# A recurrence over eight chunks: the query output of a chunk placed behind the next chunk's rounds, and the small weight renormalised second

## What is computed

```
def step(carry, xs):
    W0, W1, W2 = carry
    qi, ki, vi, li = xs
    l0, l1, l2 = (li[..., 0], li[..., 1], li[..., 2])
    gq = silu(jnp.einsum('bhd,bcd->bhc', W0, qi))
    hq = jnp.einsum('bhd,bcd->bhc', W2, qi)
    o = jnp.einsum('boh,bhc->bco', W1, gq * hq)
    gba = jnp.einsum('bhd,bcd->bhc', W0, ki)
    hbm = jnp.einsum('bhd,bcd->bhc', W2, ki)
...
    dw0, dw1, dw2 = (newton_schulz5(dw0), newton_schulz5(dw1), newton_schulz5(dw2))
    W0 = renorm(W0 + dw0, n0)
    W1 = renorm(W1 + dw1, n1)
    W2 = renorm(W2 + dw2, n2)
    return ((W0, W1, W2), o)
```

## Time and profile before

| what | value |
|---|---|
| median of 3 runs | 1986.2 us (1982.34 to 1986.29) |
| the profiled execution, its own time | 1982.01 us |
| its span, first to last instruction | 1980.3 us |
| mean granted clock of PE over the span | 0.914 of full speed |
| busy: PE, DVE, ACT, POOL | 88%, 70%, 40%, 55% of the span |

### The profile page before, as it was taken

The page is one execution under the profiler, slowest core; times in us unless marked ns, Lnnn a source line. Parts: engine busy times, 40 slices in busy tenths (PEclk is TensorE's granted clock), DMA queues, the critical chain, the costliest instruction groups (busy, mean ns, idle before and its releaser), DMA issues.

```text
span 1980.3 us, 35242 instructions
## 1 busy us (share of the span) xinstructions
PE 1745.4 (88%) x13630; PEld 948.8 (48%) x13630; DVE 1392.0 (70%) x2440; ACT 792.9 (40%) x1181; POOL 1095.0 (55%) x644
## 2 busy tenths in 40 slices
PE   4888751948999999999999999999999999995893
PEld 3666641834444444444444444444444444443482
DVE  3666654347787777887777877778778887786474
ACT  3444420533444444444444444444444444441131
POOL 2232204032777677776767767777677777682303
PEclk8886755969999999999999999999999999996897
DMA  7000000210000000000000000000000000003122
GB/s 243 4 3 3 3 1 30 62 38 1 1 1 1 1 1 1 1 1 1 1 1 1 1 1 1 1 1 1 1 1 1 1 1 1 1 1 99 32 58 60
DMA packets 41533, 32.76 MB, mean 17 GB/s; under 512 B 3604, under 2 KB 37392, under 8 KB 41368
## 3 DMA queue, kind: packets, MB, share of 16 engines
q1 hardware_dynamic: 31096, 22.12, 3.6%
q0 software_dynamic: 2048, 4.20, 0.7%
q10 hardware_dynamic: 8224, 4.19, 0.7%
HBM read 18.96 MB, written 11.53 MB: 15 GB/s over the span
## 4 chain that ended last, share of the span: by engine, by line
PE 81%; DVE 9%; issue 5%; POOL 3%; ACT 1%; DMA 1%; SPq 0%; DVEq 0%; POOLq 0%; ACTq 0%
PE psum L1781 23%; PE psum L1766 20%; PE psum L1740 8%; PE psum L1760 6%; PE psum L1407 2%; PE psum L1796 2%; PE psum L1790 2%; PE psum L1181 1%; PE psum L1713 1%; PE psum L1193 1%; PE psum L1367 1%; DVE a_mx L1945 1%; POOL a_acc L2077 1%; PE psum L1417 1%; PE psum L447 1%
## 5 line engine op out<-in xcount | busy, mean ns | idle before, releaser
L2077 POOL TENSOR_TENSOR a_acc<-a_acc,a_Pb 128x832 f32<-128x832 f32 x448 | 893.3, 1994 | 307.8 <-ACT a_Pb L1883 275.1
L1945 DVE TENSOR_REDUCE a_mx<-psum 128x2 f32<-128x1024 f32 x512 | 625.5, 1224 | 237.2 <-PE psum L1740 234.2
L1883 ACT ACTIVATE a_Pb<-psum 128x1024 f32<-128x1024 f32 x512 | 496.7, 1022 | 703.5 <-PE psum L1766 701.5
L1781 PE MATMUL psum<-a_Pb,a_Vb 128*64 128x512 f32 x2048 | 494.3, 604 | 0.0
L1996 DVE TENSOR_TENSOR a_acc<-a_acc,a_Pb 128x192 f32<-128x192 f32 x448 | 230.9, 515 | 28.9 <-ACT a_Pb L1883 5.4
L1781 PEld LDWEIGHTS psum<-a_Pb,a_Vb 128*64 128x64 f32 x2048 | 127.2, 136 | 244.7 <-issue 173.7
L1740 PE MATMUL psum<-a_Kh,a_Qh 64*128 64x512 f32 x1024 | 231.3, 447 | 8.4 <-DVE a_mx L1945 8.3
L1766 PE MATMUL psum<-a_Qh,a_Kh 64*128 64x512 f32 x1024 | 231.1, 447 | 0.0
L1766 PE MATMUL psum<-a_Ql,a_Kh 64*128 64x512 f32 x1024 | 203.8, 393 | 0.0
L1740 PEld LDWEIGHTS psum<-a_Kh,a_Qh 64*128 64x128 f32 x1024 | 97.1, 184 | 222.6 <-issue 211.6
L1766 PE MATMUL psum<-a_Qh,a_Kl 64*128 64x512 f32 x1024 | 203.4, 392 | 0.0
(11 more groups left out here) (385 smaller groups left out, 2004.0 us busy)
## 6 DMA issues: line engine op xcount, KB each, us to landing
x_rows<-zero ACTq DMA_DIRECT2D x2, 2048.0 KB, 20.9
g_w<-in_L_ffn_w_eDF_dram SPq DMA_DIRECT2D x2, 1408.0 KB, 8.7
r_W<-in_L_ffn_W_dram SPq DMA_DIRECT2D x1, 2048.0 KB, 12.4
r_tile_x<-x_rows SPq DMA_DIRECT2D x16, 128.0 KB, 2.1
y_rows<-r_tile_y SPq DMA_DIRECT2D x16, 128.0 KB, 1.8
g_tile_x<-x_rows SPq DMA_DIRECT2D x16, 128.0 KB, 2.2
y_rows<-g_tile_y SPq DMA_DIRECT2D x16, 128.0 KB, 1.8
g_w<-in_L_ffn_w_eFD_dram SPq DMA_DIRECT2D x2, 512.0 KB, 10.5
```

The lines of the kernel that those rows point to most:

```text
L1781: last = pe.matmul(ps[HEAD[h], B_O, :], b.Vb[:, p // 2 % 2, kc, at], b.Pb[:, step % BUFS, h * QT:(h + 1) * QT], start=(kc == 0), stop=(kc ...
L1883: act.activation(b.Pb[:, step % BUFS, :], ps[:, slot:slot + 2, :].rearrange("p a b -> p (a b)"), ACT.Exp, scale=SCALE).then_inc(S["probs"], 1)
L1945: v.tensor_reduce(b.mx[:, :, qc, quarter:quarter + 1], ps[:, bank:bank + 2, :], AX.X, ALU.max).then_inc(S[f"free{bank}"], 1)
L2077: g.tensor_tensor(b.acc[:, u, at], before, b.Pb[:, step % BUFS, at], ALU.add).then_inc(S["added_pool"], 1)
```

## The change

1. PE issues `forward_output(c - 1)` at the end of iteration c, behind the two matmuls of the row sums, and no longer between the query products and the gradients. W1's transposed copy `W1T` gets two buffers for this.
2. The output no longer goes from PSUM to DVE. ACT copies it to a new tile `o` (`keep_output`, L520 of the new text), after the table load that ends iteration c. POOL adds the residual in iteration c + 1, behind the scaling of queries and keys, and DVE takes the statistics (`stats(c - 2)`) in that same iteration. The products of the next chunk wait for the copy.
3. The gate of the previous chunk moves behind `db` and `hb` on ACT, and behind `dh` and `hd` on POOL. `db` and `dh` now come before `hb` and `hd`.
4. The last additions, the renormalisations and the products go in the order W0, W1, W2 (`PRODUCT_ORDER`). The rounds go in the order 0, 1, 2.
5. POOL's three products with the rates (`rate`) and the blocks are issued after the third polynomial of rounds 0, 1, 2 and 3, and no longer in a row.

The diff, cut to what the prediction speaks of:

```diff
@@ ttt_pe, products @@
             pe.wait_ge(S["w1_kept"], c)
+            if c > 1:
+                pe.wait_ge(S["output_kept"], c - 1)
...
-        for m in range(3):
+        for n, m in enumerate(PRODUCT_ORDER):
             if c:
-                pe.wait_ge(S["moved"], 3 * (c - 1) + m + 1)
+                pe.wait_ge(S["moved"], 3 * (c - 1) + n + 1)
+                if n == 1:
+                    pe.wait_ge(S["norms"], 3 * c + 2)
@@ ttt_pe, main loop @@
         query_products(c)
-        if c:
-            forward_output(c - 1)
-        pe.wait_ge(S["scaled"], c + 1)
+        pe.wait_ge(S["scaled"], 3 * c + 3)
...
         row_sums(c, 0)
         row_sums(c, 1)
+        if c:
+            forward_output(c - 1)
@@ ttt_act @@
+    def keep_output(c):
+        act.wait_ge(S["output"], c + 1)
+        if c > 1:
+            act.wait_ge(S["residual"], c - 1)
+        act.activation(t.o[:, c % 2, :], ps[:, B_OUT, 256:512], ACT.Copy).then_inc(S["output_kept"], 1)
...
     for c in range(NC - 1):
-        if c:
-            gate(c - 1)
         act.wait_ge(S["products"], 3 * c + 1)
         act.activation(t.sig[:, :, :], products_at(ps, 0), ACT.Sigmoid).then_inc(S["products_out"], 1)
         act.wait_ge(S["products"], 3 * c + 3)
+        act.activation(t.db[:, :, :], products_at(ps, 2), ACT.Copy).then_inc(S["products_out"], 1)
         act.activation(t.hb[:, :, :], products_at(ps, 1), ACT.Copy).then_inc(S["products_out"], 1)
-        act.activation(t.db[:, :, :], products_at(ps, 2), ACT.Copy).then_inc(S["products_out"], 1)
+        if c:
+            gate(c - 1)
...
         act.activation(t.warm[:, 2 + c % 2:3 + c % 2], k.eps[:, 0:1], ACT.Sigmoid)
+        if c:
+            keep_output(c - 1)
     gate(NC - 2)
+    keep_output(NC - 2)
@@ ttt_dve @@
         head_squares(c + 1)
-        if c:
-            residual(c - 1)
         scales(c + 1)
+        if c > 1:
+            stats(c - 2)
         for n, m in enumerate(NS_ORDER):
             v.wait_ge(S["grad_squares"], 3 * c + n + 1)
...
-    residual(NC - 1)
+    for c in range(NC - 3, NC):
+        stats(c)
@@ ttt_pool @@
+    def residual(c):
+        g.wait_ge(S["output_kept"], c + 1)
+        at = slice(TPC * c, TPC * c + TPC)
+        g.tensor_tensor(k.y_all[:, at, :], t.o[:, c % 2, :].rearrange("p (a b) -> p a b", a=TPC), k.x_all[:, at, :], ALU.add).then_inc(S["residual"], 1)
...
         if c:
             gate(c - 1)
...
         scale(c + 1)
-        if c < NC - 2:
-            rates(c + 1)
-        if c:
-            blocks(c)
+        if c > 1:
+            residual(c - 2)
+        for it in range(NI - 1):
+            g.wait_ge(S["G"], 15 * c + 3 * it + 3)
+            if it < 3 and c < NC - 2:
+                rate(c + 1, it)
+            if it == 3 and c:
+                blocks(c)
```

More of the change, by code:

```diff
@@ L441, in ttt_pe @@
                 pe.wait_ge(S["X"], 7 * c + 3 + it)
-                if c and it == 0:
-                    pe.wait_ge(S["residual"], c)
                 for n, m in enumerate(NS_ORDER):
@@ L455, in ttt_pe @@
                 pe.wait_ge(S["X"], 7 * c + 7)
-                for m in range(3):
-                    pe.wait_ge(S["G"], at + (1 if m == 0 else 3))
+                for n, m in enumerate(PRODUCT_ORDER):
+                    pe.wait_ge(S["G"], at + (1 if n == 0 else 3))
                     for h in range(HEADS):
@@ L613, in scales, with stats @@
         v.tensor_tensor(s2v, s2v, rb, ALU.mult).then_inc(S["scales"], 1)
-    def residual(c):
-        v.wait_ge(S["output"], c + 1)
-        v.tensor_tensor(k.y_all[:, TPC * c:TPC * c + TPC, :], ps[:, B_OUT, 256:512].rearrange("p (a b) -> p a b", a=TPC),
-                        k.x_all[:, TPC * c:TPC * c + TPC, :], ALU.add).then_inc(S["residual"], 1)
+    def stats(c):
         v.wait_ge(S["residual"], c + 1)
@@ L732, in ttt_dve @@
             dve.wait()
[L733 to L743 removed]
+            if m == 2:
+                dve.did(v.tensor_tensor(t.NR[:, at], t.NR[:, at], t.N0[:, at], ALU.mult))
+                dve.wait()
+                v.tensor_scalar(t.Wc[:, 2, :], t.Wn[:, 2, :], t.NR[:, at], None, ALU.mult).then_inc(S["moved"], 1)
+            else:
+                v.tensor_tensor(t.Wc[:, m, :], t.NR[:, at], t.WN[:, at], ALU.mult).then_inc(S["moved"], 1)
     v.wait_ge(S["q_gate"], NC)
@@ L798, in ttt_pool @@
     scale(0)
-    rates(0)
+    for part in range(3):
+        rate(0, part)
     for c in range(NC - 1):
+        g.wait_ge(S["gated"], c + 1)
+        g.wait_ge(S["products_out"], 3 * c + 2)
+        g.tensor_tensor(t.dh[:, :, :], t.db[:, :, :], t.sg[:, :, :], ALU.mult).then_inc(S["hidden"], 1)
+        g.wait_ge(S["products_out"], 3 * c + 3)
+        g.tensor_tensor(t.hd[:, :, :], t.sg[:, :, :], t.hb[:, :, :], ALU.mult).then_inc(S["hidden"], 1)
         if c:
             gate(c - 1)
-        g.wait_ge(S["gated"], c + 1)
-        g.wait_ge(S["products_out"], 3 * c + 2)
-        g.tensor_tensor(t.hd[:, :, :], t.sg[:, :, :], t.hb[:, :, :], ALU.mult).then_inc(S["hidden"], 1)
-        g.wait_ge(S["products_out"], 3 * c + 3)
-        g.tensor_tensor(t.dh[:, :, :], t.db[:, :, :], t.sg[:, :, :], ALU.mult).then_inc(S["hidden"], 1)
-        scale(c + 1)
-        if c < NC - 2:
-            rates(c + 1)
-        if c:
-            blocks(c)
+        scale(c + 1)
+        if c > 1:
+            residual(c - 2)
[5 more added lines that the diff above has]
+                blocks(c)
     gate(NC - 2)
     blocks(NC - 1)
+    for c in range(NC - 3, NC):
+        residual(c)
 def norm_dve(k, n, g, have_stats=False):
```

84 lines of the change are left out of this document (38 added, 46 removed).

## The result

The changed kernel takes 2026.75 us (median of 4 runs, 2019.28 to 2031.28) against 1984.9 us for the kernel before (4 runs, 1982.34 to 1986.29): a ratio of 1.0202, with a 95% interval of 1.0177 to 1.0227. It is slower, as forecast, but by 42 us where 1999 (range 1989 to 2010) was predicted.

The account below looks back on a forecast made before the run. The recurrence was taken as a chain of waits with no engine full. Handovers 15, chunk 1 -0.9, POOL -4.0, end +2.0, clock +3 gave +15.1: 1997 from 1982.0, 2001 against the median; forecast 1999, range 1989 to 2010 us.

Parts of the forecast that it names:

- First new wait: Handover: the next chunk's products wait for ACT's copy of the output and start 2.06 us later, ending 1.06 later.
- Second new wait: Handovers into chunks 2 to 6: DVE's statistics wait for POOL's residual, so the sums of squares start 3.1 us later.
- forecast -0.9: Handover into chunk 1: neither new wait, the small weight's multiply no longer stalls; 0.9 us gained.
- L607 behind the gate multiply: Handover: DVE's second scale step waits for POOL's last gate multiply; without this lock, 0.75 us less per handover, 3.8 in all.
- POOL's work lifted from the rounds, -4: Start of the rounds: with POOL's rates and blocks gone, DVE's steps run at their shortest; -4.0 us, bounds -2 and -5.
- The end, +2.0: After the last chunk: its gate comes 1.3 us later and the last output, over two engines, costs 0.7 more.
- The clock, +3: Rounds after PE's pause of about 4 us: first rounds at the low clock, +3 us, bounds 0 and +8.
- two such rounds: Clock term: two rounds at the low clock in each of five chunks, at 0.36 us each.
- The bound of +8: Clock term's upper bound; all five rounds of five chunks at the low clock would give 9 us, some being low already.
- slower still: Rival, chance 0.13: the pause lowers the clock in all rounds of five chunks, +8 to +9; 2003 or 2007 us.
- theory A: Follow-up theory: the pause ahead of the sums over the heads lets PE's clock fall just before the rounds, which pay.

Follow-up runs that it names:

- e5: e1 with the previous chunk's output products and their copy moved from the handover into the last round: 2009.31 us, ratio 1.0121.
- e12: e10 with 5 products of constants on PE in chunk 0, which has no output products: 1979.92 us, ratio 0.9997 (0.9969 to 1.0026).
- e3: Kernel before, nothing moved, but DVE waits in chunks 1 to 5 ahead of the gradient reduces for POOL's rate products: 2026.34 us, ratio 1.0187.
- e4: e3 with 18 products of constants on PE in the pause of chunks 1 to 5: 1999.37 us, ratio 1.0048.
- e1: Changed kernel with DVE's statistics taken behind the first round's polynomial instead of ahead of the gradient reduces: 2006.73 us, ratio 1.0087.
- e7: Kernel before with products of constants in the handover, 10 behind the row sums and 5 ahead of the third products: 1989.71 us, ratio 1.0031.
- e6: e1 with 8 products of constants on PE behind the first gradient in every chunk: 1995.26 us, ratio 1.0057.
- e8: e5 with 6 products of constants behind the row sums and 6 ahead of the sums over the heads: 1989.83 us, ratio 1.0031.
- e10: e1 with the previous chunk's output products between the first gradient's products and the sums over the heads, copied there by ACT: 1988.26 us, ratio 1.0012.

## Why the prediction was right in its sign and wrong in its size

- **First new wait.** Right. It was to put the products 4.8 us behind the first weight step (70.7, against the first L716 at 65.90); in chunk 2 it is 4.27 (102.85 - 98.58), with the output products partly at the high clock, and 4.71 in chunk 3 (140.37 - 135.66). That the output and not ACT's queue sets the copy's start was a close thing: in chunk 3 the output ends at 139.74 and ACT's last instruction before the copy at 139.70, and in chunk 2, where the output ended at 102.15, the copy starts behind ACT's, at 102.28. e5 prices the output's place in the handover at 1.9 (14.07 to 12.15).
- **Second new wait.** Right. The handover was to be 13.43 (79.33 - 65.90) + 3.1 = 16.5; it is 15.97, then 16.40 four times. Together with chunk 1 (-1.2, forecast -0.9) the handovers cost 12.8 us, forecast 14.
- **L607 behind the gate multiply.** Right: L623 takes 1.05 at the median. The trace agrees with the Trainium skill's rule of a lock on the shared ports ("SBUF — State Buffer", section "SBUF: two separate sides"): L623 ends with POOL's L801, both at 111.6.
- **POOL's work lifted from the rounds, -4.** The instructions behave as forecast, L704, L708 and L719 at 0.17, 0.16 and at most 0.26. It shortens a first round only where the clock is high: e12's chunk 1 has 2.86, the kernel before 3.61. At the low clock PE fills the round.
- **The end, +2.0.** From the last weight step's start to the last statistics' end is 16.0 us before, 16.8 after: +0.8. Of what is missing, 0.9 is luck: the last output products ran at the high clock (1.16 us against 2.07).
- **The clock, +3.** This step failed. Gradient and rounds of chunks 2 to 6 took 103.2 us against 80.6: +22.6. The prediction took "A round at 1.00 takes 2.69 (90.00 - 87.31), one at 0.50 takes 3.05 (239.92 - 236.87): 0.36 each". These are not the same round. The first holds a projection for chunk 3; the second is of chunk 6, where none is left to project. Like for like it is 2.69 against 4.41, 1.72 each, and 2.38 against 3.06 without a projection. The second fault is "two such rounds": the clock didn't come back in any round of these chunks. The bound of +8 rested on the same 0.36, and so did the rival "slower still", which named the right mechanism with a chance of 0.13 and priced it at 9.
- **Chunk 0, +5.6, and chunk 1, +1.0,** were in no sum. Chunk 0's level need not be the change's doing: in e3 and e4, whose chunk 0 is that of the kernel before, it was low too, and in that kernel's own profile it was high.
- **A small reading.** The recurrence's 227 of 1980 us are 11.5% of the time, not 13%; nothing hangs on it.

With 22.6 in place of 3 - 4 (it contains what POOL's lift gave), the same sum is 38.7, or 2021 for the profiled execution, and 2026 with chunk 0's 5.6. That execution took 2024.06.

"TensorE: Matmul & The Clock Gate" in the Trainium skill, section "HAM oscillation — how this bites in real kernels", says that a repeated wait brings the clock down each time. The traces agree: 5 of 5 chunks in the changed kernel, 5 of 5 in e3. I had cited it and left it as a rival of size; what was missing was not the rule but the price.

What stays open is what decides at a short pause. Between 0.5 and 1.3 us of idle PE, chunks with the same code came out at either level (e1: 2 of 6 high; e5: 1 of 6), and e7 was at times low with pauses of 0.75. Nor is a fall the only way to a low chunk. In e1 the clock rose ahead of the sums and fell again in chunk 2, but in chunks 1, 4 and 6 it never rose, and chunk 0 was low in ten of the fourteen profiles with no pause ahead of its sums at all. So theory A explains the chunks with the long wait, and not these. That work on PE right ahead of the rounds raises the share of high chunks is shown by e6 and e8 to e10; whether its width or its mere presence counts was not tried.

## What to carry to other kernels

Before moving work off a chain, ask what PE does in its place: a wait of 3 us cost 3 us directly and 4.5 us more in the 16 us of matmuls behind it. Price a clock change on two instances of the same stretch, with the same matmuls in it, and assume that it lasts for all of a busy stretch (here to the next handover) rather than for a round or two. Where other engines need the time, put real, non-urgent products there, as e10 did, and not constants, which at the low clock are slow themselves.

## What the hardware showed that I had not expected

- Full activity doesn't always bring the clock back. In chunk 2 of the changed kernel PE is busy 4.00 of 4.00 us in 120 to 124 and in 124 to 128 us, and stays at 0.50 until the next handover. In the kernel before, chunk 1 enters the same rounds at 1.00 (from 78 us on) and keeps it through them. But the clock can come up inside the rounds: in chunk 1 of the changed kernel it is 0.50 over 86 to 87 us and 0.95 over 87 to 88, in the first round, behind a pause of 0.58 us, and in e10's chunk 2 likewise, behind no pause. The Trainium skill's page on the clock gate, in the section "Part 1: The HAM clock gate (the "warmup" mystery)", lets a busy TensorE return to the high clock; these two chunks agree, and for the rounds behind the long pause, whose matmuls are mostly 32 and 64 wide, the measurement says no (a busy PE in these windows is one whose matmuls' ends are modelled, so it need not be at its peak). What makes the difference is not shown.
- The fall needn't be seen in the pause. In the changed kernel the clock falls while PE idles (0.80 over 112 to 116 us); in e3 it is 1.00 over 88 to 92 us, which hold nearly the whole pause, and the fall is in the work behind it. The window of the rounds is the one to read.
- One kernel's runs can lie far apart: e1's nine are between 1991 and 2015 us, the four of e3, whose profile is low in every chunk but the last, within 7 us. That the clock's level in the single chunks makes this spread is likely, at 5.6 us for a chunk, but not shown, since only one execution of each kernel has its chunks on record.
